# A fused attention and FP4 feed-forward layer: turning the FFN activations by DMA instead of on TensorE

## The reference

```python
x = _layernorm(x + attn(x)); x = _layernorm(x + ffn(x))

# attn: chunked linear recurrence with decay; as a whole
#   out + alpha * (((out @ shift(out).T) * decay_mask) @ (out @ W_write.T)) @ W_read.T

def fp4_quant_dequant(x):            # blocks of 16 along the last dim
    scale = max(max(abs(xb)) / 6.0, 1e-12)
    xn = xb / scale
    q = _GRID[searchsorted(_MID, abs(xn))] * sign(xn) * scale
def fp4_linear(x, w): return fp4_quant_dequant(x) @ fp4_quant_dequant(w).T
h = silu(fp4_linear(x, w_gate)) * fp4_linear(x, w_up)      # 256 -> 704
ffn = fp4_linear(h, w_down)                                 # 704 -> 256
```

## Time and profile before

| | us |
|---|---|
| median of 3 runs (lowest, highest) | 324.36 (324.16, 324.38) |
| span of the profiled execution | 322.5 |
| its own device time | not given apart from the runs above |
| TensorE busy | 314.5 |
| VectorE busy | 293.0 |
| GpSimd busy | 238.2 |
| ScalarE busy | 213.2 |

### The profile page before, as it was taken

How to read it: one execution, slowest core, us unless ns; L and a number is a source line. 1 busy time by engine, 2 the same in 40 slices (tenths; PEclk the granted TensorE clock), 3 DMA queues, 4 the chain that set the end, 5 groups by cost and what they waited for, 6 DMA issues and landing times.

```text
span 322.5 us, 6519 instructions
## 1 busy us (share of the span) xinstructions
PE 314.5 (97%) x2067; PEld 285.2 (88%) x2067; DVE 293.0 (91%) x746; ACT 213.2 (66%) x521; POOL 238.2 (74%) x258
## 2 busy tenths in 40 slices
PE   7999999999999999999999999999999999999994
PEld 3999988989998998999989998898989889998983
DVE  4799789989899999899998999889999999999973
ACT  7769994767775647844784556766675555665664
POOL 1999898668696868676886768777779588368872
PEclk9999999999999999999999999999999999999999
DMA  6830301010010200320020200021000000001002
GB/s 227 302 125 9 132 0 67 1 66 2 1 67 16 84 16 0 100 82 3 16 83 17 83 17 3 33 65 35 1 18 17 16 18 17 19 16 35 17 33 84
DMA packets 8242, 15.69 MB, mean 49 GB/s; under 512 B 1040, under 2 KB 5136, under 8 KB 8208
## 3 DMA queue, kind: packets, MB, share of 16 engines
q1 hardware_dynamic: 7920, 15.01, 14.0%
q10 hardware_dynamic: 288, 0.26, 0.3%
HBM read 11.08 MB, written 4.19 MB: 47 GB/s over the span
## 4 chain that ended last, share of the span: by engine, by line
PE 69%; DVE 17%; issue 5%; ACT 4%; POOL 3%; ACTq 0%; DVEq 0%; POOLq 0%
PE gu L1712 11%; PE gu L1716 11%; PE gu L1713 11%; PE bank L1817 5%; PE bank L1712 4%; PE bank L1716 4%; PE bank L1713 4%; PE bank L1722 3%; DVE h_y L1094 3%; PE bank L1725 3%; PE bank L1726 3%; DVE w_raw L1209 2%; DVE hqT_lo L1236 2%; DVE h_am L1215 2%; PE bank L1783 2%
## 5 line engine op out<-in xcount | busy, mean ns | idle before, releaser
L413 POOL TENSOR_TENSOR h_q<-h_g,h_ns 128x704 f32<-128x704 f32 x32 | 51.2, 1604 | 47.7 <-DVE h_g L1099 47.6
L1712 PE MATMUL gu<-guT_hi,xqT_hi 128*128 128x512 f32 (+1 forms) x192 | 74.0, 386 | 0.7 <-DVE w_raw L1209 0.6
L1713 PE MATMUL gu<-guT_lo,xqT_hi 128*128 128x512 f32 (+1 forms) x192 | 72.2, 376 | 0.0
L1716 PE MATMUL gu<-guT_hi,xqT_lo 128*128 128x512 f32 (+1 forms) x192 | 56.6, 376 | 0.0
L699 ACT ACTIVATE w_raw<-gu 128x512 f32<-128x512 f32 x64 | 29.3, 462 | 32.7 <-PE gu L1716 32.4
L406 POOL TENSOR_TENSOR h_n<-w_raw,h_rs 128x704 f32<-128x704 f32 x32 | 47.0, 1472 | 3.4 <-DVE h_rs L1089 3.2
L719 ACT CAST hqT_hi<-bank 128x512 fp32r<-128x512 f32 x64 | 30.4, 478 | 17.7 <-PE bank L1817 17.2
L1712 PEld LDWEIGHTS gu<-guT_hi,xqT_hi 128*128 128x128 f32 x192 | 36.1, 188 | 6.0 <-ACT xqT_hi L688 0.9
L1716 PEld LDWEIGHTS gu<-guT_hi,xqT_lo 128*128 128x128 f32 x192 | 35.5, 188 | 6.0 <-ACT xqT_lo L693 0.2
L1713 PEld LDWEIGHTS gu<-guT_lo,xqT_hi 128*128 128x128 f32 x192 | 36.1, 188 | 4.8
L1094 DVE SCALAR_TENSOR_TENSOR h_y<-h_sq,h_n 128x704 f32<-128x704 bf16 x34 | 36.9, 1090 | 0.0
(11 more groups left out here) (159 smaller groups left out, 936.7 us busy)
## 6 DMA issues: line engine op xcount, KB each, us to landing
xs<-in_x_rows_dram SPq DMA_DIRECT2D x8, 512.0 KB, 3.4
out_dram<-wq_gu SPq DMA_DIRECT2D x32, 128.0 KB, 1.7
x_full<-in_xt_rows_dram SPq DMA_DIRECT2D x7, 512.0 KB, 3.2
w_raw<-in_w_ffn_dram SPq DMA_DIRECT2D x6, 352.0 KB, 6.0
w_pair<-in_w_attn_dram SPq DMA_DIRECT2D x1, 512.0 KB, 5.2
x_full<-in_xt_rows_dram SPq DMA_DIRECT2D x1, 256.0 KB, 2.6
x_full<-in_xt_rows_dram ACTq DMA_DIRECT2D x1, 256.0 KB, 3.4
scal<-in_scalars_dram ACTq DMA_DIRECT2D x1, 1.0 KB, 1.7
```

Of the source, the lines that this page charges most:

```text
L413: nc.gpsimd.tensor_tensor(blocks(h_q[:, p, 0:I]), blocks(h_g[:, p, :]), per_block(h_ns[:, p, :], HB), ALU.mult).then_inc(h_quant, 1)
L1712: nc.tensor.matmul(dst, lh, rh, start=(first and i == 0), stop=False)
L1713: nc.tensor.matmul(dst, lh, rl, start=False, stop=False)
L1716: last = nc.tensor.matmul(dst, ll, rh, start=False, stop=(end and i == len(terms) - 1))
```

## The change

Tiles 0 to 29 no longer transpose h on TensorE; tiles 30 and 31 keep the old way. The grid values (before the scale is applied) are written as bfloat16, repeated to 768 columns and transposed by a DMA from SBUF to SBUF. The scales of the tile (56 columns: eight blocks per 128 columns, by seven columns, of which six are used) are transposed by one TensorE operation, copied to SBUF by ScalarE, written to DRAM and read back by a DMA that repeats each row 16 times. GpSimd then multiplies the two, already transposed.

```diff
+def write_h_scales(k, p, turn):      # SP
+    sp.wait_ge(hs_copied, k + 1)
+    sp.dma_start(h_scales_dram[k], h_s[:, p, :]).then_inc(hs_written[p], 16)
+def spread_h_scales(k, p, turn):     # SP
+    sp.wait_ge(hs_written[p], 16 * turn)
+    if turn > 1: sp.wait_ge(h_quant, k - 1)
+    sp.dma_start(h_sT[:, p, :], over_rows(h_scales_dram[k], SC, HC)).then_inc(hs_landed[p], 16)
+def turn_h_grid(k, p, turn):         # SP
+    sp.wait_ge(hg_repeated, k + 1)
+    if turn > 1: sp.wait_ge(h_quant, k - 1)
+    sp.dma_start_transpose(h_gT[:, p, :, :], h_g[:, p, :]).then_inc(hg_turned[p], 16)
+def over_rows(rows, held, used):
+    return rows.rearrange("(k c) t -> k (c t)", c=held)[:, 0:used * P].unsqueeze(1).to_broadcast((KB, BLK, used * P))
 
-    nc.gpsimd.tensor_tensor(blocks(h_q[:, p, 0:I]), blocks(h_g[:, p, :]), per_block(h_ns[:, p, :], HB), ALU.mult)
+def h_spread(k, p, turn):            # GpSimd
+    pool.wait_ge(hs_landed[p], 16 * turn); pool.wait_ge(hg_turned[p], 16 * turn)
+    pool.wait_ge(hT_lo_ready, 2 * k - 2)          # k >= 2
+    nc.gpsimd.tensor_tensor(h_q[:, p, :], h_gT[:, p, :, :].rearrange("p c t -> p (c t)"), h_sT[:, p, :], ALU.mult)
 
+def repeat_h_scales(k, p):           # ScalarE, 4 elements a row
+def copy_h_scales(k, p, turn):       # ScalarE
+    nc.scalar.copy(h_s[:, p, :], ps[0:SROWS, hs_at[k], 0:P]).then_inc(hs_copied, 1)
+def hg_repeat(k, p):                 # ScalarE, bfloat16, 64 columns; in place of h_repeat
+def h_round_all(k, p):               # ScalarE; in place of two h_round out of PSUM
+    nc.scalar.copy(hqT_hi[:, p, :], h_q[:, p, :]).then_inc(hT_hi_ready, 2)
+def h_rest_all(k, p):                # VectorE; in place of two h_rest
+    nc.vector.tensor_tensor(hqT_lo[:, p, :], h_q[:, p, :], hqT_hi[:, p, :].bitcast(F32), ALU.subtract)
+def h_scale_rows(k, p, free):        # TensorE; in place of two h_transpose
+    nc.tensor.transpose(ps[0:SROWS, hs_at[k], 0:P], h_ns[:, p, :], ident[:]).then_inc(hs_filled, 1)
 
 # h_to_grid(k), k >= 2: VectorE waits for the transpose of k - 2
+    dve.wait_ge(hg_turned[p], 16 * (k // 2))
```

```diff
-nc.scalar.activation(h_sq[:, p, :], h_n[:, p, :], ACT.Square, scale=ROOT_K)
+nc.scalar.activation(two_banks(h_sq_at[k]), halves(h_n[:, p, :]), ACT.Square, scale=ROOT_K)
```

**Scale operations in odd row counts.** h_ns has seven columns per group of blocks, h_am two further rows of ones. `x_moments` works on one column at a time, `out_moments` leaves the mean column to GpSimd:

```diff
 # x_moments
-nc.vector.tensor_scalar(z_nm[:, c], z_sum[:, c], -1.0 / D, None, ALU.mult)
-nc.vector.tensor_scalar(z_ve[:, c], z_ssq[:, c], 1.0 / D ** 3, LN_EPS, ALU.mult, ALU.add)
+for i in (2 * u, 2 * u + 1):
+    nc.vector.tensor_scalar(z_nm[:, i:i + 1], z_sum[:, i:i + 1], -1.0 / D, None, ALU.mult)
+    last = nc.vector.tensor_scalar(z_ve[:, i:i + 1], z_ssq[:, i:i + 1], 1.0 / D ** 3, LN_EPS, ALU.mult, ALU.add)
 # out_rstd -> out_stats
-nc.gpsimd.tensor_tensor(o_shift[:, c], o_nm[:, c], o_rstd[:, c], ALU.mult)
+nc.gpsimd.tensor_scalar(o_shift[:, c], o_sum[:, c], o_rstd[:, c], -1.0 / D, ALU.mult, ALU.mult)
```

**Smaller edits.** `v_subtract`, `v_remainder`, `xq_subtract` and `xq_remainder` are gone (4 and 2 times); VectorE's `v_rest` and `xq_rest` do these too. `gate_up` waits only for silu_ready before it fills the gate bank, and for h_ready before the up bank:

```diff
-    pe.wait_ge(h_ready, 2 * k + half - 1)
+    pe.wait_ge(h_ready if half else silu_ready, 2 * k + half - 1)
 for m in range(2 - half):
+    if k >= 1 and m == 1: pe.wait_ge(h_ready, 2 * k - 1)
```

More of the change, by code:

```diff
@@ L1494, in _ @@
-            run(body)
-            h_magic_add(16, 0)
+            xq_rest(2, 1)
+            h_magic_add(5, 1)
+            h_to_grid(5, 1)
+            hidden(8, 0, 0)
+            h_magic_add(6, 0)
+            v_rest(3, 1)
+            h_to_grid(6, 0)
+            hidden(8, 0, 1)
+            h_maxima(8, 0)
+            x_residual(3, 0)
+            h_divisors(7, 1)
+            h_divisors(8, 0)
+            h_reciprocals(7, 1)
+            x_moments(3, 0)
+            h_reciprocals(8, 0)
+            out_residual(0, 0)
@@ new lines, in _ @@
+            xq_rest(3, 0)
+            x_magic_add(3, 1)
+            h_rest_all(4, 0)
+            out_residual(2, 2)
+            out_residual(3, 3)
+            hidden(11, 1, 1)
+            x_to_grid(3, 1)
+            out_moments(2, 0)
+            h_maxima(11, 1)
+            h_to_grid(9, 1)
+            out_moments(3, 1)
+            h_rest_all(5, 1)
+            out_residual(4, 0)
+            xq_rest(3, 1)
+            h_rest_all(6, 0)
+            x_residual(4, 0)
+            out_moments(4, 0)
@@ new lines, in _ @@
+            x_divisors(4, 0)
+            out_moments(6, 0)
+            x_reciprocals(4, 0)
+            h_rest_all(7, 1)
+            h_magic_add(10, 0)
+            h_to_grid(10, 0)
+            x_magic_add(4, 0)
+            x_residual(4, 1)
+            x_to_grid(4, 0)
+            h_magic_add(11, 1)
+            decay_scores(5, 0)
+            h_to_grid(11, 1)
+            x_moments(4, 1)
+            hidden(13, 1, 0)
+            hidden(13, 1, 1)
+            v_rest(5, 0)
+            xq_rest(4, 0)
@@ new lines, in _ @@
+            decay_scores(5, 1)
+            decay_scores(5, 2)
+            h_maxima(13, 1)
+            decay_scores(5, 3)
+            h_divisors(13, 1)
+            h_reciprocals(13, 1)
+            x_maxima(4, 1)
+            v_rest(5, 1)
+            x_divisors(4, 1)
+            x_reciprocals(4, 1)
+            out_residual(7, 3)
+            h_rest_all(8, 0)
+            h_magic_add(12, 0)
+            x_residual(5, 0)
+            h_to_grid(12, 0)
+            out_moments(7, 1)
+            x_moments(5, 0)
@@ L1572, in _ @@
+            out_residual(15, 3)
+            out_moments(14, 0)
+            decay_scores(7, 3)
+            h_rest_all(16, 0)
+            h_rest_all(17, 1)
+            v_rest(7, 0)
+            x_magic_add(6, 1)
+            v_rest(7, 1)
             x_to_grid(6, 1)
-            h_rest(19, 3, 0)
-            hidden(23, 1, 0)
-            x_moments(7, 1)
             hidden(23, 1, 1)
-            out_residual(18, 2)
-            h_rest(19, 3, 1)
+            h_to_grid(21, 1)
+            h_magic_add(22, 0)
@@ L1976, in _ @@
[L1976 to L1981 removed]
+            gate_up(7, 1, 3, 1)
+            h_scale_rows(4, 0, [(wT_lo_ready, 8)])
+            values(3, 0, [(hs_copied, 4)])
+            xq_transpose(2, 0, [(hs_copied, 5)])
+            scores(3, 0, [(x_grid, 6)])
+            scores(3, 1, [(wT_lo_ready, 9)])
+            xq_transpose(2, 1, [(v_lo_ready, 7)])
@@ new lines, in _ @@
+            scores(3, 2, [(x_grid, 5)])
+            gate_up(8, 2, 0, 0)
+            values(3, 1, [(xqT_lo_ready, 6)])
+            gate_up(8, 2, 0, 1)
+            gate_up(9, 2, 1, 0)
+            reads(3, 0, [(h_grid, 7)])
+            gate_up(9, 2, 1, 1)
+            h_scale_rows(5, 1, [(z_ready, 7)])
+            h_scale_rows(6, 0, [(h_grid, 7)])
+            pe.wait_ge(wT_lo_ready, 9)
+            down(0, 0, [(v_lo_ready, 8)])
+            h_scale_rows(7, 1, [(hs_copied, 7)])
+            scores(3, 3, [(hs_copied, 6)])
```

2325 lines of the change are left out of this document (1347 added, 978 removed).

## The result

The changed kernel takes 336.17 us in the median of 4 runs (335.67 to 340.25), the kernel before 324.37 beside it: ratio 1.039, 95% interval 1.034 to 1.045. It is slower by 11.8 us where I forecast 12.0 us faster. The profiled execution took 336.12 us with a span of 334.2, so 1.9 us lie around the span again.

A forecast was written before the change was run, and what follows sets the result against it. TensorE's end-to-end sequence was taken as the bound, with VectorE just under. 322.5 - 13.5 + 1.0 + 0.5 = 310.5 us span, 312.4 us measured with 1.9 us around it; range 306 to 324.

The forecast's parts named there:

- the cover of the new path: DMA path per tile: 7.0 us of grid, repeat, transpose and spread hidden within two tiles, 18.8 us.
- The scale branch (1.7 + some 3 us) runs beside it: Scales' write to DRAM and read back, 1.7 + some 3 us, run beside the 4.4 us transposing DMA.
- The new waits for banks: TensorE waits behind VectorE and ScalarE for shared PSUM banks: 0.5 us added, range 0 to 10.
- the hole that I had counted: Transposes of tiles 27 to 29 lie behind the last gate_up, so removing their 2.0 us shortens nothing.
- the last chain: Small steps of tile 31 after the last gate_up; tile 29's transpose can delay them 0 to 4.4 us, 1.0 taken.
- the two small terms: Added to the span: 1.0 us delay in tile 31's final steps and 0.5 us for TensorE's bank waits.
- TensorE's own sequence: TensorE's work, laid end to end, sets the time; before the last gate_up it loses 17.5 + 1.4 - 5.4 = 13.5 us.
- The transpose: Transposing DMA of 192 KB per tile: 768 packets at 91 ns over 16 engines, 4.4 us.
- The rival that the contention stays: VectorE's contention with GpSimd does not leave with squares in PSUM; 315 to 322 us, no separate chance given.
- Slower, mild: TensorE's in-order waits on the longer scale loop cost over 0.4 us a tile; at 0.7 us, 333; chance 0.08.
- Slow transposes: Transposing DMAs, all in one queue, set the pace above 9.8 us a turn; at 12 us, 390 us; chance 0.08.
- The first rival: VectorE, or the order, becomes the bound, with only VectorE freeing the squares' banks; 315 to 322 us, chance 0.16.

The follow-up runs named there:

- the version with all three repairs: Changed kernel with scales written twice and spread from 16 rows, three start steps in old order, and h_g four deep: 320.66 us, ratio 0.989.
- three steps put back: Changed kernel with scores(0, 0) before combine, x_round(0, 1) before decay_mask, x_rest(0, 1) before w_maxima(0), as in the old order: 333.72 us, ratio 1.028.
- the one without the turn: Changed kernel without the transposing DMA, h_spread reading h_g untransposed, and also h_g four deep instead of two; output not the layer's: 324.11 us, ratio 0.998.

## Why the prediction was wrong

**The failed step is the cover of the new path**: "Hidden by: tile k+2 uses the buffers of k, that is two tiles, 2 x 301/32 = 18.8 us; grid, repeat, transpose and spread are 0.9 + 0.2 + 4.4 + 1.5 = 7.0." Both numbers are wrong for this kernel. In the trace after, h_g(k+2) starts 5.6 to 29.6 us after h_g(k), 16.8 in the mean, since the order sets tiles unevenly. And from the start of the grid to the end of h_spread it takes 9.1 to 37.3 us, 22.1 in the mean; in 19 of 30 tiles it is over 18.8. That count of 19 shows that the sum was wrong, not what the excess cost: with constant scales 16 of 30 are over 18.8, and that kernel takes 318 us. What must fit is narrower. h_g is held until its turn has landed, 4.1 to 24.9 us after the grid's start, 11.1 in the mean, and in five tiles (2, 6, 17, 18 and 22) that filled the whole distance; those are VectorE's five waits, 9.2 us. In the kernel before, from the grid's start to the end of h_dequant, which frees h_g there, is 3.0 us in the mean, at distances of 10.0 to 23.9. I summed durations of operations; what fills the time is their place in the queues of SP and GpSimd, each of which stands for the other (6.7 us in the mean from grid to the issue of the turn, up to 20.7, though the repeat between takes 0.2). The consequence I did write down, "h_to_grid of k+2 waits on VectorE for hg_turned with everything queued behind it there", and priced at nothing. The four-deep h_g shows its price, as long as the scale branch is slow: 9.6 us.

**"The scale branch (1.7 + some 3 us) runs beside it"** failed in size. Write and spread follow each other, 3.3 + 5.9 = 9.2 us in the mean, up to 6.9 and 7.4, against 4.7 forecast and against the 4.4 of the turn beside it. The write shares the queue with transfers of 384 and 512 KB, and the spread, by its updates, ran on half of the engines. Widening it brought 9.3 us, removing the branch 18.1. The two failed steps are not separate losses to be added: without the branch VectorE never stood before h_g, and four-deep h_g and wide spread overlap.

**"The new waits for banks ... I add 0.5 (0 to 10)"** was the term in which both should have stood. The standing rose by 28.2 us. Of that, 2.0 us is the hole that I had counted (the transposes of tiles 27 to 29, removed from the shadow of the last chain) and 1.5 the two small terms; 24.7 were not forecast. The other side was right: TensorE's own sequence lost 16.9 us, against 13.5 + 2.0 = 15.5. With the 0.4 us at the very end: 24.7 - 1.4 + 0.4 = 23.7, which is 334.2 - 310.5.

**The transpose** was sized rightly, but by luck: 4.4 us taken, 4.4 in the mean, 4.2 in the median, 2.7 to 7.0. The trace has the 768 packets a turn of my working (23,040 of 256 bytes in all), but one took 44 ns in the mean, not 91, which makes 2.1 us; with constant scales it took 25 ns, and the turn still landed in 2.8 us in the median and 3.1 in the mean. So part of the landing is not the pieces, and part is the traffic beside it. The Trainium skill, "Advanced Engine Details and Errata", section "X-Bar Transpose (TRN2)", states that transposing DMAs are as fast as ordinary ones, at 350 to 400 GB/s, an estimate of 0.5 to 0.6 us for 192 KB; no turn here landed in under 2.7 us.

**VectorE** came out at 278.6 us against 276.5, h_y at 877 ns (886 forecast), x_y at 680 (684), h_rest_all at 1082 (950 to 1170). The rival that the contention stays is refuted by the squares put back: h_y 1225 ns. The Trainium skill, "SBUF — State Buffer", section "Who interferes with whom", says that a VectorE instruction with two inputs in SBUF contends with a GpSimd instruction that reads SBUF, and one with at most one such input, outside the two-port modes, does not. The traces agree: h_y took 825 to 893 ns with its squares in PSUM and up to 2189 with both inputs in SBUF, and h_rest_all, with both in SBUF, 957 in the median and up to 1873.

**The last chain.** It was to begin near 288 us; the last gate_up handed over at 310.07, and in the version with all three repairs at 295.8.

**The rivals.** "Slower, mild" had the time (333) and a chance of 0.08; it named TensorE's in-order waits on the scale loop. That is half of it: TensorE rarely waited for the scales themselves (1.3 us once, for h_s). It waited for VectorE, and VectorE and GpSimd for the DMAs. "Slow transposes" was wrong in its mechanism: no turn took over 7.0 us to land, against the 9.8 of its break-even. The first rival counted work, and neither engine was full; but its remark that only VectorE frees the banks of the squares came true, as TensorE's waits for h_g are waits for such banks (2.7, 1.6 and 1.3 us).

**The start** was not priced at all. In the first 60 us the standing is 11.7 us, 4.9 before, and with neither DMA path 10.3; three steps put back bring 2.4. Some 5.5 us remain there (10.4 against 4.9), and their cause is open; the waits that make up most of them are named at that run. Open as well: how much of what is left in mid-run would go with a deeper h_gT or h_sT, which wasn't tried.

## What to carry to other kernels

Don't hide a path behind "two tiles at the average pace": take the shortest distance between the two uses of a buffer from the order, and add to the path the place of each step in its engine's and queue's order, above all where step k waits for k-2 in two queues. When a full engine is relieved and the kernel slows, look first at which neighbour now stands before a buffer; a deeper buffer (9.6 us here) was worth as much as a spread that lands in 4.4 instead of 5.9 us (9.3), though the two overlap. When a run changes two things at once, as the one without the turn did, run the smaller one alone before you price the other. A transfer that broadcasts is worth a look at how many rows its source has.

## What had not been expected of the hardware

- The spread of 384 KB from 8 source rows took 5.9 us in the mean with 9 semaphore updates; from 16 rows 4.4 us with 16, although it moved the same bytes and 28 KB more were written.
- A write of 28 KB took 1.4 to 6.9 us to land; under the same load stores of 128 KB went from 1.7 us to 2.9. Issued from ScalarE it was no faster in the mean (3.3 us both ways).
- A transposing DMA of 192 KB took its issuing queue 1.24 us in the mean in the changed kernel (1.21 to 1.46), a store of 128 KB 0.40, a write of 28 KB 0.43, a spread of 384 KB 0.60.
- With the squares in SBUF, GpSimd's own work rose from 239.5 to 267.2 us: the contention costs both sides.
